# A state-space scan's softplus: the logarithm of 1 + u as a degree-nine polynomial, in the place of a reciprocal and an odd series

## The chip, the cores and the metric

The kernel runs on one core of one Trainium2 chip. The metric is device time in microseconds (us), of one execution of the whole program. It is the median of several runs.

A core has five engines that are used here, each with a queue of its own that it works through in order: TensorE (PE; its weight loads are shown as PEld), VectorE (DVE), ScalarE (ACT), GpSimd (POOL), and SyncE (SP), which only issues transfers here. They wait for one another by semaphores.

## What is computed

A decoder of four layers with twelve stages runs over x of 8 x 256 x 128 (float32). Each stage adds its result to x and normalises. The change is in the seventh stage, a selective state-space scan:

```python
def _L2_attn_ref(x, W_in, b_in, W_dt1, b_dt1, W_dt2, b_dt2, A, D):
    BC = x @ W_in + b_in                                  # N = 16 states
    Bm, Cm = (BC[..., :N], BC[..., N:])
    dt = jax.nn.softplus((x @ W_dt1 + b_dt1) @ W_dt2 + b_dt2)
    dt = jnp.clip(dt, 1e-07, 1000000.0)
    tmp = A * dt[..., None]
    A_bar = jnp.exp(tmp)
    B_barX = jnp.expm1(tmp) / tmp * dt[..., None] * Bm[:, :, None, :] * x[..., None]
    # h[s] = A_bar[s] * h[s-1] + B_barX[s], an associative scan along the sequence
    return jnp.sum(h * Cm[:, :, None, :], axis=-1) + D * x
```

The softplus of z is max(z, 0) + log(1 + u) with u = exp(-|z|), a number between 0 and 1.

## The kernel before

Each engine's program is written out by hand: for each stage a function gives this engine's instructions in their order, and semaphores named after the stage tie the engines together. The feed-forward stage ahead of the scan is `L1f`, the scan is `L2a`, and the next one is `L2x`.

**Tiling of the scan.** There are 8 batch rows b. For each, 128 channels lie on the partitions and 256 positions along the free dimension. The 16 states are taken in four chunks of four, so a chunk is a tile of 128 x 1024, and there are 32 chunks t = 4b + c. All engines' functions loop over `t in range(SCAN_FIRST, SCAN_LAST)`.

For each chunk, ACT scales x by B (`scaled`, L2288, eight instructions), PE transposes that into PSUM (`inputs`, L1729), and ACT makes the decay and half of the gain from the step size (`decays`, L2274 and L2275, eight instructions). DVE then forms the rest of the gain's factor (`feed`, L3091, reading `big` and PSUM), POOL multiplies (`gains`, L823 and L824), and DVE runs the scan (`scan`, L3099) and multiplies its result by C (L3103), which PE had spread over partitions in PSUM (`spread_c`, L1742). PE sums over the states (`summed`, L1758).

**Once per batch row**, ahead of need, the step size is made: PE projects (`scan_turn_x` L1645, `scan_project` L1650 and L1651, `scan_step_sizes` L1656 and L1658), ACT copies (L2227, L2237, L2238), and DVE adds the bias and so makes z (`scan_sized`, L2994 and L2997). ACT makes u (`scan_small_exponential`, L2245 and L2247), DVE makes the logarithm in two parts (`scan_ratio`, L3006 to L3009, and `scan_series`, L3014 to L3017), and then the softplus and its bounds (`scan_softplus`, L3031 to L3033). DVE also adds the residual and normalises (`residual` L3108, `deviations` L3114 and L3117, `norm` L3123).

`due(t, offset, 4)` gives the b for which t = 4b + offset. With the constants `SCAN_RATIO` = -6, `SCAN_SERIES` = -4 and `SCAN_DT` = -3, the ratio of row b stands behind the chunk 4b - 6, the series behind 4b - 4, and the softplus ahead of `feed` in the round 4b - 3. So DVE has two heavier rounds in each four: that with the ratio, and that with the series and the softplus. Row 0 is an exception: its whole logarithm and softplus stand at the end of `L1f`, and row 1's ratio ahead of the first `feed`.

`line.step(...)` is an instruction on DVE and a wait, also on DVE, for its end; `line.did(...)` is one without the wait. The ratio of the series is s = u / (u + 2), since log(1 + u) = 2 (s + s^3/3 + s^5/5 + ...); q is s squared, `s_of` is in the tile `resb`, `q_of` in `KT`, `series` in `xs`, and u in `OT`.

## Time and profile before

| | |
|---|---|
| median of 3 runs | 1869.52 us (1866.8 to 1877.95) |
| the profiled execution | 1869.56 us, of which the profile's span is 1867.8 us |
| PE busy | 1581.1 us, 85% of the span |
| DVE busy | 1295.2 us, 69% |
| ACT busy | 1055.6 us, 57% |
| POOL busy | 651.8 us, 35% |
| chain that ended last | PE 47%, DVE 23%, POOL 11%, issue 9%, ACT 8%, DMA 2% |

All times of an instruction are read from one profiled execution, counted from the start of its span. "Busy" is the time in which at least one instruction of an engine ran. Matmuls are pipelined and their ends are modelled, so that a busy PE is not one at its peak. PEclk is the clock that TensorE was granted, as a share of 2.4 GHz: 1.00 is that, and 0.50 is 1.2 GHz. The chain that ended last is followed back from the last instruction: at each step to what released it, or to the instruction before it on its engine. "[idle <- X]" behind an instruction is the time its engine had been idle before it, and the instruction that ended the idle time. The scan's part of the span lies between about 784 us, where the last rows of `L1f` overlap it, and 1040.5 us.

### The profile page before, as it was taken

To read this page: it belongs to the slowest core of one execution; us is meant where nothing else is said; L and a number is where in the kernel's file an instruction comes from. 1 tells how busy PE (TensorE), PEld (TensorE's weight loads), DVE (VectorE), ACT (ScalarE), POOL (GpSimd) and SP (SyncE) were. 2 spreads that over 40 slices of the span, in tenths; PEclk is the share of its full clock that TensorE was granted. 3 is DMA by queue.
4 is the path that set the end of the run, shared out by engine and by line. 5 is a ranking of instruction groups with operands and counts; after the bars stand their busy time and mean duration, and the time that the engine had idled before them with its cause. 6 is when DMAs were issued, how large, how long until landed. Compare 5 with 4: busy or idle time off the path is not lost.

```text
span 1867.8 us, 34707 instructions
## 1 busy us (share of the span) xinstructions
PE 1581.1 (85%) x12844; PEld 1135.7 (61%) x12847; DVE 1295.2 (69%) x2889; ACT 1055.6 (57%) x2177; POOL 651.8 (35%) x750
## 2 busy tenths in 40 slices
PE   6488857689998888889988899998899997978875
PEld 5244436568876555668777666665559974655542
DVE  2678862387776885679999467748844457468877
ACT  4388842267764775278787155537744442047645
POOL 3355525488884022445666213220000010001223
PEclk9699977899999999967888899999979998999985
DMA  3200121200000000000000100000000000000000
GB/s 118 109 13 12 35 86 34 57 10 1 1 1 1 2 2 1 4 34 1 1 1 1 55 2 2 2 12 1 2 1 1 1 10 1 1 18 2 2 1 23
DMA packets 14792, 30.95 MB, mean 17 GB/s; under 512 B 1537, under 2 KB 10145, under 8 KB 13857
## 3 DMA queue, kind: packets, MB, share of 16 engines
q1 hardware_dynamic: 13602, 26.63, 4.2%
q0 software_dynamic: 1024, 2.10, 0.4%
q8 instruction: 104, 1.70, 0.4%
q14 instruction: 62, 0.51, 0.1%
HBM read 22.42 MB, written 6.29 MB: 15 GB/s over the span
## 4 chain that ended last, share of the span: by engine, by line
PE 47%; DVE 23%; POOL 11%; issue 9%; ACT 8%; DMA 2%; SPq 0%; DVEq 0%; POOLq 0%; ACTq 0%
PE PS L1294 5%; PE PS L1354 4%; DVE negmax L2547 4%; POOL big L803 4%; DVE V L3099 3%; PE PS L1596 3%; PE PS L1607 3%; POOL big L791 3%; PE PS L1376 3%; ACT big L2066 2%; POOL big L799 2%; PE PS L1299 2%; ACT big L2044 2%; PE PS L1350 2%; PE PS L1368 2%
## 5 line engine op out<-in xcount | busy, mean ns | idle before, releaser
L2044 ACT ACTIVATE big<-PS 128x1024 f32<-128x1024 f32 (+1 forms) x256 | 248.2, 971 | 171.8 <-PE PS L1305 171.2
L2547 DVE TENSOR_REDUCE negmax<-PS 128x4 f32<-128x1024 f32 x192 | 234.9, 1224 | 59.3 <-PE PS L1294 58.2
L687 POOL TENSOR_TENSOR rstd<-veps,mhalf 128x2 f32<-128x2 f32 x72 | 51.7, 717 | 423.4 <-DVE veps L2430 423.0
L1294 PE MATMUL PS<-KS,QS 32*128 32x256 f32 (+1 forms) x1152 | 135.4, 320 | 50.3 <-DVE negmax L2547 37.1
L1294 PEld LDWEIGHTS PS<-KS,QS 32*128 32x128 f32 x1152 | 88.2, 189 | 127.3 <-DVE negmax L2547 88.7
L1354 PE MATMUL PS<-big,V 128*32 128x256 f32 (+1 forms) x2048 | 139.1, 392 | 0.7 <-ACT big L2044 0.4
L1305 PE MATMUL PS<-QS,KS 32*128 32x256 f32 (+1 forms) x1152 | 137.1, 326 | 0.6 <-ACT big L2044 0.6
L713 POOL TENSOR_TENSOR res<-resb,XB 128x256 f32<-128x256 f32 x24 | 17.4, 725 | 279.0 <-ACT resb L2130 279.0
L2566 DVE SCALAR_TENSOR_TENSOR QT<-PS,wint 128x1024 f32<-128x1024 f32 x64 | 77.2, 1219 | 30.1 <-PE PS L1247 30.0
L1305 PEld LDWEIGHTS PS<-QS,KS 32*128 32x128 f32 x1152 | 87.2, 192 | 6.0 <-issue 4.9
L755 POOL TENSOR_SCALAR KT<-QT 128x1024 f32<-128x1024 f32 x64 | 66.6, 1041 | 69.0 <-DVE QT L2566 67.1
L1758 PE MATMUL PS<-On,V 128*128 128x128 f32 x512 | 89.8, 348 | 0.8 <-DVE V L3103 0.8
L1758 PEld LDWEIGHTS PS<-On,V 128*128 128x128 f32 x512 | 83.3, 255 | 10.3 <-issue 9.3
L2209 ACT ACTIVATE QT<-PS,W 128x256 f32<-128x256 f32 x128 | 53.5, 470 | 59.4 <-PE PS L1596 59.4
L1376 PE MATMUL PS<-causal,identb 128*128 128x256 bf16 x595 | 85.9, 287 | 0.0
L1350 PE MATMUL PS<-big,V 128*32 128x512 f32 x512 | 67.7, 649 | 20.9 <-ACT big L2066 11.6
L1354 PEld LDWEIGHTS PS<-big,V 128*32 128x32 f32 x2048 | 55.4, 113 | 46.9 <-issue 18.7
L803 POOL TENSOR_TENSOR big<-big 128x512 f32<-128x512 f32 x64 | 81.2, 1269 | 5.0
L1023 PE MATMUL PS<-OT,W 128*128 128x256 f32 x272 | 73.3, 391 | 10.6 <-ACT QT L2001 10.6
L791 POOL TENSOR_SCALAR big<-big,rsum 128x256 f32<-128x256 f32 (+1 forms) x144 | 60.5, 432 | 62.4 <-DVE rsum L2477 62.3
L2288 ACT ACTIVATE QT<-x_tok,rt 128x128 f32<-128x128 f32 x256 | 77.8, 386 | 6.2 <-PE PS L1729 3.7
L1742 PE MATMUL PS<-OT,SEL 16*128 16x256 f32 x256 | 70.5, 418 | 11.6 <-DVE V L3103 11.6
(443 smaller groups left out, 4300.6 us busy)
## 6 DMA issues: line engine op xcount, KB each, us to landing
W<-in_wpack SPq DMA_DIRECT2D x1, 4180.0 KB, 12.3
W<-in_wpack SPq DMA_DIRECT2D x1, 2560.0 KB, 9.0
W<-in_wpack SPq DMA_DIRECT2D x1, 2449.5 KB, 9.6
y_rows<-one_more SPq DMA_DIRECT2D x1, 2048.0 KB, 10.6
masks<-in_mask SPq DMA_DIRECT2D x8, 256.0 KB, 2.8
x_rows<-x_tok SPq DMA_DIRECT2D x16, 128.0 KB, 2.0
W<-in_wpack SPq DMA_DIRECT2D x1, 1538.0 KB, 6.1
x_tok<-in_x SPq DMA_DIRECT2D x1, 1024.0 KB, 5.2
```

The costliest lines, as they stand in the source:

```text
L791: ins = nc.gpsimd.tensor_scalar(PRW[:, u % 4, c0:c1], PRW[:, u % 4, c0:c1], rsum[:, u % 16, j:j + 1], 1.0, ALU.mult, ALU.mult)
L803: nc.gpsimd.tensor_tensor(q, q, RTW[:, u % 4, :, :], ALU.add).then_inc(sem("t_rope"), 1)
L1294: mm = nc.tensor.matmul(PS[:, MAXB[half], o], QS[r, bm % 2, tm, j * P:(j + 1) * P], KS[r, bm % 2, tm, k], start=not a.causal, stop=last)
L1305: mm = nc.tensor.matmul(PS[:, exp_banks(ge)[half], o], KS[r, be % 2, te, kb * P:(kb + 1) * P], QS[r, be % 2, te, q], start=not a.causal, s ...
L1350: mm = nc.tensor.matmul(out_rows.rearrange("p (k c) -> p k c", k=2), v, PX_BOTH[:, :, T % 2, h, kb * S:(kb + 1) * S], start=first, stop=last)
L1354: mm = nc.tensor.matmul(out_rows[:, skip:S], v, PX[:, T % 2, h, kb * S:(kb + 1) * S - skip], start=first, stop=last)
L1376: nc.tensor.matmul(PS[:, bank, 0:S], identb[:, :], causal[:, 0, :], start=True, stop=True)
L1758: mm = nc.tensor.matmul(PS[:, YB, j * P:(j + 1) * P], chunk("h", t)[:, at:at + P], by_state[:, 4 * c + k, :], start=False, stop=c == 3 and ...
L2044: nc.scalar.activation(PX[:, T % 2, 2 * p:2 * p + 2, 0:cols], PS[:, exp_banks(g)[0]:exp_banks(g)[0] + 2, 0:cols], ACT.Exp, scale=a.scale). ...
L2288: ins = nc.scalar.activation(chunk("x", t)[:, at:at + P], x_tok[:, 2 * b + j, :], ACT.Copy, scale=B_cols(b)[:, i:i + 1])
L2547: ins = nc.vector.tensor_reduce(negmax[:, h:h + 2, :].rearrange("p h j -> p (h j)"), banks.rearrange("p h (j k) -> p (h j) k", j=2), AX.X, ...
L2566: nc.vector.scalar_tensor_tensor(clipped(QT, g), PS[:, pair_banks(g):pair_banks(g) + 2, :], -100.0 / a.scale, capT[:, g // PAIRS % 2, :].u ...
```

## The change

The logarithm is now a polynomial of degree nine in u itself, without a constant term. Two instructions give u * (c9 * u) and + c8 * u, and eight more each add a coefficient and multiply by u: ten instructions of the form SCALAR_TENSOR_TENSOR on 128 x 256, in place of four for the ratio (one of them a RECIPROCAL) and seven for the series. `scan_softplus` loses the instruction that formed 2s + s * series (L3031). The first five stand where the ratio was (`scan_logarithm_high`), and the other five where the series was (`scan_logarithm_low`). The separate increment of the semaphore `L2a_series` (L3017) is gone; the last of the ten increments it. u has two buffers in turn (the old tile in `OT`, and the place of q in `KT`), and ACT's wait before it writes u is for the polynomial of row b - 2 in place of the ratio of row b - 1. The intermediate tile `xT` and the places of s and q are no longer used here. Nothing else is changed on any engine.

```diff
@@ -220,6 +220,9 @@
 MASKED = -2.0 ** 100
 TURN_X_STEP, V_STEP, OT_STEP, Y_STEP = 6, 7, 2, 3
 STAGES = ORDER
+
+LOG1P = (0.999999994656, -0.499998926481, 0.333297104989, -0.249516162628, 0.196632742569,
+         -0.152696670739, 0.10543623795, -0.0563736128301, 0.0195425272629, -0.0031760570192)
 TURNED = [s for s in ORDER if s in ATTNS and ATTNS[s].turned_scores]
 
 
@@ -507,8 +510,11 @@
         def z_of(b):
             return OT[:, 6 + b % 2, :]
 
-        low_rank, u_of = OT[0:64, 4, :], OT[:, 5, :]
-        s_of, q_of, series = resb[:, :, :].rearrange("p j c -> p (j c)"), KT[:, 6, :], xs[:, :, :].rearrange("p j c -> p (j c)")
+        low_rank, series = OT[0:64, 4, :], xs[:, :, :].rearrange("p j c -> p (j c)")
+
+        def u_of(b):
+            return (OT[:, 5, :], KT[:, 6, :])[b % 2]
+
         diag, most = KT[:, 7, 0:P], KT[:, 7, P:P + 1]
         by_state = On[:, :, :].rearrange("p j (n c) -> p (j n) c", n=8)
 
@@ -2240,11 +2246,11 @@
 
             def scan_small_exponential(b):
                 act.wait_ge(sem("L2a_zdt"), b + 1)
-                if b:
-                    act.wait_ge(sem("L2a_q"), b)
-                nc.scalar.activation(u_of, z_of(b), ACT.Abs).then_inc(sem("L2a_absz"), 1)
+                if b >= 2:
+                    act.wait_ge(sem("L2a_series"), b - 1)
+                nc.scalar.activation(u_of(b), z_of(b), ACT.Abs).then_inc(sem("L2a_absz"), 1)
                 act.wait_ge(sem("L2a_absz"), b + 1)
-                nc.scalar.activation(u_of, u_of, ACT.Exp, scale=-1.0).then_inc(sem("L2a_u"), 1)
+                nc.scalar.activation(u_of(b), u_of(b), ACT.Exp, scale=-1.0).then_inc(sem("L2a_u"), 1)
 
             def L1f():
                 n = "L1f"
@@ -2996,25 +3002,22 @@
                                         w("L2a_brow").unsqueeze(1).broadcast_to([P, 2, 16]), ALU.add)
                 nc.vector.tensor_scalar(z_of(b), PS[:, 7, 0:S], w("L2a_bdt2"), None, ALU.add).then_inc(sem("L2a_zdt"), 1)
 
-            def scan_ratio(b):
+            def scan_logarithm_high(b):
 
 
                 dve.wait_ge(sem("L2a_u"), b + 1)
-                if b:
-                    dve.wait_ge(sem("L2a_series"), b)
-                s1 = xT[:, :]
-                line.step(nc.vector.scalar_tensor_tensor(s1, u_of, 2.0, u_of, ALU.add, ALU.max))
-                line.step(nc.vector.reciprocal(s1, s1))
-                line.step(nc.vector.tensor_tensor(s_of, u_of, s1, ALU.mult))
-                nc.vector.tensor_tensor(q_of, s_of, s_of, ALU.mult).then_inc(sem("L2a_q"), 1)
-
-            def scan_series(b):
-
-                dve.wait_ge(sem("L2a_q"), b + 1)
-                line.step(nc.vector.tensor_scalar(series, q_of, 2.0 / 15, None, ALU.mult))
-                for k in (13, 11, 9, 7, 5, 3):
-                    line.step(nc.vector.scalar_tensor_tensor(series, series, 2.0 / k, q_of, ALU.add, ALU.mult))
-                dve.sem_inc(sem("L2a_series"), 1)
+                u = u_of(b)
+                line.step(nc.vector.scalar_tensor_tensor(series, u, LOG1P[9], u, ALU.mult, ALU.mult))
+                line.step(nc.vector.scalar_tensor_tensor(series, u, LOG1P[8], series, ALU.mult, ALU.add))
+                for k in (7, 6, 5):
+                    line.step(nc.vector.scalar_tensor_tensor(series, series, LOG1P[k], u, ALU.add, ALU.mult))
+
+            def scan_logarithm_low(b):
+
+                u = u_of(b)
+                for k in (4, 3, 2, 1):
+                    line.step(nc.vector.scalar_tensor_tensor(series, series, LOG1P[k], u, ALU.add, ALU.mult))
+                nc.vector.scalar_tensor_tensor(series, series, LOG1P[0], u, ALU.add, ALU.mult).then_inc(sem("L2a_series"), 1)
 
             def scan_constants():
                 dve.wait_ge(*loaded("L2a"))
@@ -3028,8 +3031,7 @@
                 dve.wait_ge(sem("L2a_series"), b + 1)
                 if b >= 2:
                     dve.wait_ge(sem("L2a_decay"), 4 * (b - 1))
-                line.step(nc.vector.scalar_tensor_tensor(s_of, series, 2.0, s_of, ALU.add, ALU.mult))
-                line.step(nc.vector.scalar_tensor_tensor(z_of(b), z_of(b), 0.0, s_of, ALU.max, ALU.add))
+                line.step(nc.vector.scalar_tensor_tensor(z_of(b), z_of(b), 0.0, series, ALU.max, ALU.add))
                 nc.vector.scalar_tensor_tensor(step_size(b), z_of(b), 1e-7, most.broadcast_to([P, S]), ALU.max, ALU.min)\
                   .then_inc(sem("L2a_dt"), 1)
 
@@ -3074,8 +3076,8 @@
                         scan_constants()
                     elif b == 5:
                         scan_sized(0)
-                scan_ratio(0)
-                scan_series(0)
+                scan_logarithm_high(0)
+                scan_logarithm_low(0)
                 scan_softplus(0)
                 residual(B - 1)
 
@@ -3140,9 +3142,9 @@
                     if (b := due(t, SCAN_STEP_SIZE, 4)) is not None:
                         scan_sized(b)
                     if b := due(t, SCAN_RATIO, 4):
-                        scan_ratio(b)
+                        scan_logarithm_high(b)
                     if b := due(t, SCAN_SERIES, 4):
-                        scan_series(b)
+                        scan_logarithm_low(b)
                     if (b := due(t, SCAN_Y, 4)) is not None:
                         deviations(b)
 
```

In the listings below each row is an instruction of DVE's program: its line, its operation, the tile it writes <- those that it reads, its size, and how many like it follow one another. `xs` is the tile of the series or polynomial, `OT` and `KT` hold u, z and the step size, `resb` s, `V` the scan's result, `PS` is PSUM, `big`, `wint` and `one_more` hold decays, gains and their factors. Lines of the changed kernel are shifted: L3091 is now L3093, L3099 is L3101, L3103 is L3105, L3123 is L3125, L3108 is L3110.

DVE at the end of `L1f`, where row 0's logarithm and softplus are made, before:

```order
L3006 SCALAR_TENSOR_TENSOR xT<-OT 128x256
L3007 RECIPROCAL xT<-xT 128x256
L3008 TENSOR_TENSOR resb<-OT,xT 128x256
L3009 TENSOR_TENSOR KT<-resb 128x256
L3014 TENSOR_SCALAR xs<-KT 128x256
L3016 SCALAR_TENSOR_TENSOR xs<-xs,KT 128x256 x6
L3031 SCALAR_TENSOR_TENSOR resb<-xs,resb 128x256
L3032 SCALAR_TENSOR_TENSOR OT<-OT,resb 128x256
L3033 SCALAR_TENSOR_TENSOR KT<-OT,KT 128x256
```

The same place after the change:

```order
L3010 SCALAR_TENSOR_TENSOR xs<-OT 128x256
L3011 SCALAR_TENSOR_TENSOR xs<-OT,xs 128x256
L3013 SCALAR_TENSOR_TENSOR xs<-xs,OT 128x256 x3
L3019 SCALAR_TENSOR_TENSOR xs<-xs,OT 128x256 x4
L3020 SCALAR_TENSOR_TENSOR xs<-xs,OT 128x256
L3034 SCALAR_TENSOR_TENSOR OT<-OT,xs 128x256
L3035 SCALAR_TENSOR_TENSOR KT<-OT,KT 128x256
```

Fourteen instructions became twelve, and the reciprocal is gone; nothing moved past anything else.

DVE inside the scan, in the round of four that has the ratio (from the end of one chunk to the next `feed`), before:

```order
L3099 SCALAR_TENSOR_TENSOR V<-big 128x1024
L3103 TENSOR_TENSOR V<-V,PS 128x1024
L3006 SCALAR_TENSOR_TENSOR xT<-OT 128x256
L3007 RECIPROCAL xT<-xT 128x256
L3008 TENSOR_TENSOR resb<-OT,xT 128x256
L3009 TENSOR_TENSOR KT<-resb 128x256
L3123 SCALAR_TENSOR_TENSOR x_tok<-res,mv,rstd 128x128 x2
L3091 SCALAR_TENSOR_TENSOR one_more<-big,PS 128x1024
```

And after the change:

```order
L3101 SCALAR_TENSOR_TENSOR V<-big 128x1024
L3105 TENSOR_TENSOR V<-V,PS 128x1024
L3010 SCALAR_TENSOR_TENSOR xs<-KT 128x256
L3011 SCALAR_TENSOR_TENSOR xs<-KT,xs 128x256
L3013 SCALAR_TENSOR_TENSOR xs<-xs,KT 128x256 x3
L3125 SCALAR_TENSOR_TENSOR x_tok<-res,mv,rstd 128x128 x2
L3093 SCALAR_TENSOR_TENSOR one_more<-big,PS 128x1024
```

Four instructions became five, at the same place in the queue.

DVE in the round of four that has the series and the softplus, before:

```order
L3103 TENSOR_TENSOR V<-V,PS 128x1024
L3014 TENSOR_SCALAR xs<-KT 128x256
L3016 SCALAR_TENSOR_TENSOR xs<-xs,KT 128x256 x6
L3108 TENSOR_TENSOR res<-PS,x_tok 128x256
L3031 SCALAR_TENSOR_TENSOR resb<-xs,resb 128x256
L3032 SCALAR_TENSOR_TENSOR OT<-OT,resb 128x256
L3033 SCALAR_TENSOR_TENSOR KT<-OT,KT 128x256
```

And after the change:

```order
L3105 TENSOR_TENSOR V<-V,PS 128x1024
L3019 SCALAR_TENSOR_TENSOR xs<-xs,OT 128x256 x4
L3020 SCALAR_TENSOR_TENSOR xs<-xs,OT 128x256
L3110 TENSOR_TENSOR res<-PS,x_tok 128x256
L3034 SCALAR_TENSOR_TENSOR OT<-OT,xs 128x256
L3035 SCALAR_TENSOR_TENSOR KT<-OT,KT 128x256
```

Ten instructions and a separate increment became seven.

## Rows read from the trace of the kernel before

**Rows 1.** Busy time in a stretch: start:end, length, engines, PEclk, DMA, GB/s; the scan.
```profile
790.00:1040.50 250.50, 220.70 (x1134) 183.37 (x1134) 229.03 (x288) 188.11 (x538) 141.56 (x81) 0.79 0.02 7
```

**Rows 2.** The same view (PE, PEld, DVE, ACT, POOL): two rounds of four, then others.
```profile
883.65:913.27 29.62, 27.99 (x141) 23.61 (x140) 28.86 (x36) 22.47 (x66) 17.97 (x10) 0.77 0.00 1
913.27:942.89 29.62, 27.72 (x148) 23.49 (x147) 28.86 (x36) 25.70 (x75) 17.97 (x10) 0.80 0.00 1
1001.65:1023.23 21.58, 18.55 (x119) 16.32 (x120) 20.56 (x21) 18.06 (x50) 17.98 (x10) 0.92 0.00 1
808.00:828.00 20.00, 20.00 (x72) 15.94 (x71) 14.55 (x19) 17.32 (x51) 9.75 (x5) 0.51 0.01 1
```

**Rows 3.** Groups of DVE instructions by form, 853 to 972: busy, mean ns | idle.
```profile
L3103 DVE TENSOR_TENSOR V<-V,PS 128x1024 f32<-128x1024 f32 x16 | 19.5, 1221 | 0.6
```

**Rows 4.** Waits from 853 to 972: total us, times, longest.
```profile
ACT OT L2245 <- DVE OT L2997: 12.6, 4, 4.0
PE PS L1742 <- DVE V L3103: 4.5, 6, 1.6
```

**Rows 5.** Timeline of DVE, start and duration: the round with series and softplus.
```profile
877.93 1.15 DVE L3014 TENSOR_SCALAR xs<-KT 128x256 f32<-128x256 f32 x1
879.12 2.72 DVE L3016 SCALAR_TENSOR_TENSOR xs<-xs,KT 128x256 f32<-128x256 f32 x6
882.05 0.42 DVE L3108 TENSOR_TENSOR res<-PS,x_tok 128x256 f32<-128x256 f32 x1 [0.21 <-DVE xs L3016]
882.39 0.41 DVE L3031 SCALAR_TENSOR_TENSOR resb<-xs,resb 128x256 f32<-128x256 f32 x1
...
882.84 0.43 DVE L3032 SCALAR_TENSOR_TENSOR OT<-OT,resb 128x256 f32<-128x256 f32 x1
...
883.64 1.22 DVE L3091 SCALAR_TENSOR_TENSOR one_more<-big,PS 128x1024 f32<-128x1024 f32 x1
```

**Rows 6.** The chain that ended last, in order of time: two steps of the series.
```profile
880.03 0.44 DVE xs L3016
880.49 0.44 DVE xs L3016
```

**Rows 7.** Timeline of DVE and POOL: the round with the ratio.
```profile
890.01 2.28 DVE L3099 TENSOR_TENSOR_SCAN V<-big 128x1024 f32<-128x1024 f32 x1
...
890.28 4.18 POOL L824 TENSOR_TENSOR big<-big,wint 128x1024 f32<-128x1024 f32 x1
...
893.47 1.28 DVE L3006 SCALAR_TENSOR_TENSOR xT<-OT 128x256 f32<-128x256 f32 x1
...
894.78 1.75 DVE L3007 RECIPROCAL xT<-xT 128x256 f32<-128x256 f32 x1
...
897.37 0.61 DVE L3123 SCALAR_TENSOR_TENSOR x_tok<-res,mv,rstd 128x128 f32<-128x128 f32 x2
```

**Rows 8.** Timeline at the end of the stage before: row 0's logarithm and softplus.
```profile
785.43 0.42 DVE L3006 SCALAR_TENSOR_TENSOR xT<-OT 128x256 f32<-128x256 f32 x1
...
792.70 0.42 DVE L3033 SCALAR_TENSOR_TENSOR KT<-OT,KT 128x256 f32<-128x256 f32 x1
...
793.16 0.51 ACT L2274 ACTIVATE big<-KT,W 128x256 f32<-128x256 f32 x1 [3.37 <-DVE KT L3033]
```

**Rows 9.** Chain that ended last: one chunk's transposes, spreading and summing at PEclk 0.50.
```profile
813.18 3.71 PE PS L1742 x8
816.89 1.90 PE PS L1729 x8
...
824.07 3.41 PE PS L1758 x16
```

**Rows 10.** Timeline of DVE: where it waits for PE in the first chunks.
```profile
811.43 0.19 DVE L2994 TENSOR_TENSOR rt<-PS,W 128x32 f32<-128x32 f32 x1 [3.98 <-PE PS L1658]
...
832.23 1.22 DVE L3103 TENSOR_TENSOR V<-V,PS 128x1024 f32<-128x1024 f32 x1 [1.01 <-PE PS L1742]
...
843.99 4.00 DVE L3099 TENSOR_TENSOR_SCAN V<-big 128x1024 f32<-128x1024 f32 x1 [0.62 <-PE PS L1758]
```

## The prediction

> **What bounds the kernel now.** I first looked at where the changed instructions run. All of them are in the scan or in the last 5 us ahead of it, and the scan is 250.5 us of a span of 1867.8 us [rows 1]. Whatever the rest of the kernel is bound by, the change acts through the scan's length alone.
>
> Within the scan the busy times are PE 220.70, DVE 229.03, ACT 188.11 and POOL 141.56 us [rows 1]. DVE leads only a little, so the average decides nothing. I read it in pieces of one batch row (four chunks). From about 854 us on, such a piece takes 29.6 us, and DVE is busy for 28.86 us of it [rows 2]. The groups of DVE's instructions from 853 to 972 us show next to no idle time: 0.6 us over sixteen of L3103 [rows 3]. The waits point the same way: ACT waits 3.1 us per batch row for DVE's z (12.6 us in 4), and PE waits for DVE's scan result [rows 4]. So DVE sets this part's pace, up to about 1001 us. PE is a close second: 27.7 to 28.0 us busy in the same pieces, at a granted clock of 0.77 to 0.80.
>
> The first chunks are different. From 808 to 828 us PE is busy for all of 20.00 us at a granted clock of 0.51, DVE for 14.55 us [rows 2], and DVE waits for PE there: 3.98, 1.01 and 0.62 us [rows 10]. Before that, at 793 us, ACT stands still for 3.37 us until DVE's row-0 softplus is there [rows 8].
>
> **The change on DVE, per batch row.** The series ran from the start of L3014 at 877.93 to the residual at 882.05: 4.12 us [rows 5]. In this are six steps, and 0.21 us idle around the separate increment. A step that waits for the one before it takes 0.46 us from start to start (880.03 to 880.49) [rows 6]; an instruction of this size that nothing waits for gives way after 0.34 us (882.05 to 882.39) [rows 5]. The ratio ran from 893.47 to 897.37: 3.90 us [rows 7]. The softplus ran from 882.39 to 883.64: 1.25 us [rows 5].
>
> The first instruction of both parts is not at its own cost. L3006 took 1.28 us there [rows 7] and 0.42 us in row 0 [rows 8]. POOL's multiplication began at 890.28, behind the scan that had begun at 890.01, and ended at 894.46 [rows 7]. L3006 began at 893.47 and came to its end just behind that. I take it that an instruction with two SBUF inputs must wait for POOL's. The new first instructions also have two SBUF inputs, so they inherit this cost: 1.31 us to the next start (893.47 to 894.78). The Trainium skill ("SBUF — State Buffer", "SBUF: two separate sides") says that VectorE and GpSimd take a shared pair of ports exclusively, for the whole of an instruction, and that both an instruction in a two-port mode and one with two SBUF inputs are held. The trace agrees for L3006, and L3014 with its 1.15 us is the first kind.
>
> New cost of the first half: 1.31 + 4 x 0.46 = 3.15 us, saving 0.75. Of the second half: 1.31 + 3 x 0.46 + 0.34 = 3.03 us, saving 1.09. Of the softplus: 0.46 + 0.34 = 0.80 us, saving 0.45. Together 2.29 us of 29.62 in a batch row.
>
> All new instructions have a shape and form that the trace shows (L3016, L3006), so 0.42 us is a measured cost. The Trainium skill ("Vector Engine (DVE) Microarchitecture Reference", "Points that are easy to get wrong") says that this form with two SBUF sources that aren't bfloat16 runs at half throughput. This would speak against the change, which has two more of them per row (twelve for ten): at an estimated 0.27 us each (256 columns at 0.96 GHz, by the skill's "VectorE: DVE Perf Modes"), the saving would be 1.75 us instead of 2.29. But TENSOR_TENSOR L3108 and L3016 take the same 0.42 to 0.45 us here, so the row decides.
>
> **Where it counts.**
> - Row 0, at the end of the stage before: L3006 starts at 785.43 and L3033 at 792.70, 7.27 us [rows 8]. New: eleven steps of 0.46, or 5.06 us. ACT stands waiting for exactly this, so 2.21 us are on the path.
> - Row 1's first half (0.75) lies ahead of the first feed, and DVE then waits 3.98 us for PE [rows 10]. Row 1's second half (1.54 with the softplus) and row 2's first half (0.75) end in chunks in which DVE waits for PE at 832 and 844 us. I count these 3.04 us as nothing. They are covered by PE's work at the low clock.
> - Rows 2 to 7, second half and softplus: 6 x 1.54 = 9.24 us. Rows 3 to 7, first half: 5 x 0.75 = 3.75 us. All lie between 849 and 1001 us, where DVE sets the pace.
>
> Together 15.2 us.
>
> **ACT's changed wait and second buffer** cost nothing. ACT waited there for z anyway (3.1 us per row) [rows 4], and the new wait is for a polynomial that ended a whole batch row earlier. The old one was not late either.
>
> **What takes some of it back.** With 27.3 us per batch row, the others have less room. ACT needs at most 25.70 us [rows 2]. PE needs 27.7 to 28.0 at a clock of 0.77 to 0.80: more than the new period, if the clock stays. But at 0.92 it did four chunks in 21.58 us, with 18.55 busy [rows 2]; they lack only the projections of the next batch row. So PE at the high level has room, and at the low level it hasn't: one chunk then takes 3.71 + 1.90 + 3.41 = 9.02 us [rows 9] against 6.84 of DVE's. I expect DVE to wait now and then behind a stretch at 1.2 GHz. Such a wait can cost more than itself. At 843.99 the scan began 0.62 us late, came behind POOL's multiplication and took 4.00 us instead of 2.28 [rows 10, 7], 1.72 us more. The bounds are nothing (the clock rises with the denser work), and 8 us (such a wait of 0.62 + 1.72 us in three or four of the six batch rows). I take one, 2 us in round numbers, since the other clusters of low clock between 854 and 972 us made DVE wait for only 0.6 us in sixteen chunks.
>
> The Trainium skill ("TensorE: Matmul & The Clock Gate", "Part 1: The HAM clock gate") says that sustained activity releases the clock's throttle. By it the denser work would bring the high level, and the 2 us would fall away. The trace bears that out only in part: 0.92 in the dense piece from 1001.65, but 0.51 from 808 to 828 us, with PE busy all the time.
>
> Sum: 15.2 - 2 = 13.2 us. The profiled execution took 1869.56 us, practically the median (1869.52), so 1856.4, rounded to 1856 us, or 0.7% less.
>
> **Rivals.**
> - A, a chance of 14%: PE or ACT takes over. DVE's gain is mostly turned into waiting, because PE is at 28 of 29.6 us. What stays is row 0's 2.2 us and up to 5 more: 1862 to 1868 us. For it speaks the low clock of 0.77. Against it, PE itself waits for DVE, 4.5 us at L1742 in four batch rows, and keeps up.
> - B, 9%: the whole gain and the covered 3.0 us as well, 18.2 us, and the 2.2 us that row 0 gives let one more piece of the PE-bound start run at the high level. Going from 9.02 to about half of that in a chunk saves up to 4 us. This gives 1848 to 1851 us.
> - C, slower, 4%: the low clock, which held from 808 to 828 us, goes on further, since other work now falls at other times. Each chunk at the low level costs 9.02 us against the new 6.84, so 2.18 us of the gain. It decides from seven chunks more than now: 7 x 2.18 = 15.3 us. With ten more it would be 1876 us, and from sixteen on over 1% slower. Against it, the stretches at the low level were short once DVE set the pace.
> - That the change doesn't do what it says is hardly possible: fourteen dependent instructions become twelve on the engine that is busy for 28.86 of 29.62 us.
>
> **How the numbers follow.** The forecast, a gain of 8 to 18 us, has 73%. With A's and B's nearer parts, the range 1850 to 1866 us leaves out less than 2 in 10. About 1% (18.7 us) is what a measurement of this kernel can tell from no change. Beyond it on the fast side is almost only B, 9%. On the slow side is only C's far end, 2%. Within 1% is 89%.
>
> **What would show it.** In the new trace: ten instructions of 0.42 us, of which the first of each half takes 1.28 us inside the scan; the series' and residual's distance 3.0 us instead of 4.1; a batch row in 27.3 us, from `feed` to the fourth `feed` after it; ACT's wait for row 0's softplus about 1.2 us instead of 3.4; and the scan's last chunk about 13 us earlier. I'm wrong if the batch rows stay near 29 us with new DVE waits for L1742, L1758 or ACT's L2275, if scans of 4 us come up often, if a new instruction takes much more than 0.42 us, or if the granted clock of the scan changes from 0.79 by much.

## The result, and the profile after

| | before | after |
|---|---|---|
| median | 1873.74 us (4 runs, 1866.8 to 1884.34) | 1850.34 us (4 runs, 1842.41 to 1861.94) |
| ratio | | 0.9877, 95% interval 0.9834 to 0.9921 |
| profiled execution | 1869.56 us | 1852.06 us, span 1850.2 us |
| PE / DVE / ACT / POOL busy | 1581.1 / 1295.2 / 1055.6 / 651.8 us | 1560.4 / 1279.8 / 1056.8 / 653.3 us |

The changed kernel is 1.2% faster, some 23 us; a fourth run of the kernel before brought its median from 1869.52 to 1873.74 us. The prediction said 1856 us, 0.7% less than 1869.52, and a gain of 8 to 18 us. The measured 1850.34 us lies 0.34 us inside the lower end of its range (1850 to 1866), and the gain lies outside the 8 to 18 us.

The instructions cost what was predicted. This is the timeline of DVE (start, duration, instruction) after the change, first the round of four with the first half of the polynomial, then the one with the second half and the softplus:

```profile
895.00 1.28 DVE L3010 SCALAR_TENSOR_TENSOR xs<-OT 128x256 f32<-128x256 f32 x1
896.31 0.43 DVE L3011 SCALAR_TENSOR_TENSOR xs<-OT,xs 128x256 f32<-128x256 f32 x1
896.77 1.34 DVE L3013 SCALAR_TENSOR_TENSOR xs<-xs,OT 128x256 f32<-128x256 f32 x3
898.14 0.61 DVE L3125 SCALAR_TENSOR_TENSOR x_tok<-res,mv,rstd 128x128 f32<-128x128 f32 x2
...
908.34 2.67 DVE L3019 SCALAR_TENSOR_TENSOR xs<-xs,OT 128x256 f32<-128x256 f32 x4
911.04 0.43 DVE L3020 SCALAR_TENSOR_TENSOR xs<-xs,OT 128x256 f32<-128x256 f32 x1
911.38 0.42 DVE L3110 TENSOR_TENSOR res<-PS,x_tok 128x256 f32<-128x256 f32 x1
911.72 0.42 DVE L3034 SCALAR_TENSOR_TENSOR OT<-OT,xs 128x256 f32<-128x256 f32 x1
912.17 0.42 DVE L3035 SCALAR_TENSOR_TENSOR KT<-OT,KT 128x256 f32<-128x256 f32 x1
912.51 1.21 DVE L3093 SCALAR_TENSOR_TENSOR one_more<-big,PS 128x1024 f32<-128x1024 f32 x1
```

From 895.00 to 898.14 are 3.14 us (3.90 before, [rows 7]), from 908.34 to 911.38 are 3.04 us (4.12, [rows 5]), and from 911.72 to 912.51 are 0.79 us (1.25, [rows 5]). Together 6.97 us instead of 9.27.

Row 0 at the end of the stage before, on ACT and DVE, to be read against [rows 8]:

```profile
794.70 0.42 DVE L3010 SCALAR_TENSOR_TENSOR xs<-OT 128x256 f32<-128x256 f32 x1
795.15 0.56 DVE L3011 SCALAR_TENSOR_TENSOR xs<-OT,xs 128x256 f32<-128x256 f32 x1
...
800.01 0.42 DVE L3035 SCALAR_TENSOR_TENSOR KT<-OT,KT 128x256 f32<-128x256 f32 x1
...
800.47 0.51 ACT L2280 ACTIVATE big<-KT,W 128x256 f32<-128x256 f32 x1 [1.41 <-DVE KT L3035]
```

ACT's wait is down from 3.37 to 1.41 us. From the first instruction to the start of the last are 5.31 us instead of 7.27.

**Where the time went.** I divided both profiled executions at the same five events: the first instruction of row 0's logarithm, the first scan instruction (L3099 before, L3101 after; `TENSOR_TENSOR_SCAN` in the profile, though the listings ahead print it as `SCALAR_TENSOR_TENSOR`), the fifth, the twenty-ninth and the last. These are stretches of before (start:end, length, PE, PEld, DVE, ACT and POOL busy with counts, PEclk, DMA share, GB/s), and one batch row:

```profile
785.43:814.44 29.01, 15.92 (x61) 10.70 (x62) 17.97 (x47) 17.43 (x51) 6.48 (x7) 0.66 0.15 55
814.44:843.99 29.55, 29.55 (x120) 24.05 (x120) 26.57 (x29) 24.63 (x73) 17.77 (x10) 0.62 0.00 1
843.99:1018.50 174.51, 158.13 (x852) 133.34 (x851) 170.03 (x202) 146.91 (x422) 105.43 (x59) 0.83 0.00 1
1018.50:1034.35 15.85, 14.96 (x86) 12.90 (x86) 14.86 (x16) 1.59 (x4) 13.66 (x8) 0.89 0.01 2
874.47:904.10 29.63, 26.68 (x150) 22.53 (x151) 28.86 (x36) 24.04 (x70) 17.97 (x10) 0.88 0.00 1
```

And the same of after:

```profile
794.70:821.50 26.80, 15.67 (x60) 10.80 (x61) 15.38 (x47) 17.43 (x51) 6.76 (x7) 0.68 0.16 59
821.50:850.21 28.71, 28.71 (x131) 23.25 (x131) 25.93 (x28) 24.05 (x70) 15.33 (x8) 0.70 0.01 1
850.21:1010.88 160.67, 139.81 (x842) 115.31 (x841) 156.82 (x191) 146.51 (x421) 107.89 (x60) 0.93 0.00 1
1010.88:1026.52 15.64, 14.97 (x86) 12.90 (x86) 14.88 (x16) 2.55 (x7) 13.67 (x8) 0.89 0.01 1
877.56:904.89 27.33, 25.32 (x149) 20.75 (x148) 26.67 (x35) 24.16 (x70) 17.97 (x10) 0.90 0.00 1
```

The four differences are 2.21, 0.84, 13.84 and 0.21 us, or 17.1 us in all. A batch row takes 27.33 us, as worked out, and DVE is busy for 26.67 of it. DVE still sets the pace: from 853 to 990 us it waited 1.0 us for PE's L1748, while PE waited 15.0 us for DVE at the same line (waits of after: total us, times, longest):

```profile
PE PS L1748 <- DVE V L3105: 15.0, 9, 2.4
```

So it was PE's waiting that grew, and not DVE's: in the window of [rows 4], from 853 to 972 us, PE's wait for DVE at this line went from 4.5 to 12.6 us. The granted clock rose too: 0.93 instead of 0.83 in the long stretch. The clock doesn't set the length of these rows: before and pad have rows of 29.6 us at clocks from 0.69 to 0.88, the four profiles of after rows of 27.3 us at clocks from 0.88 to 0.97.

What the scan doesn't explain is that the first log instruction comes 9.3 us later in this execution of after, and that 9.8 us less lie behind the last scan. The code in both places is the same. The experiments had to tell whether this is chance.

### The profile page after: what moved, and what is told of

Read it like the earlier page. It is cut to its first block, busy times and chain, and to the rows that moved or that the text cites. A ratio compares the mean times of both kernels' runs of the same rounds, so it can differ in the third digit from the quotient of the medians.

```text
span 1850.2 us, 34682 instructions
## 1 busy us (share of the span) xinstructions
PE 1560.4 (84%) x12844; PEld 1115.3 (60%) x12847; DVE 1279.8 (69%) x2873; ACT 1056.8 (57%) x2177; POOL 653.3 (35%) x750
## 4 chain that ended last, share of the span: by engine, by line
PE 47%; DVE 22%; POOL 11%; issue 9%; ACT 9%; DMA 2%; SPq 0%; DVEq 0%; POOLq 0%; ACTq 0%
PE PS L1300 5%; PE PS L1360 4%; DVE negmax L2553 4%; POOL big L809 3%; PE PS L1602 3%; PE PS L1613 3%; DVE V L3101 3%; POOL big L797 3%; PE PS L1382 3%; PE PS L1356 2%; ACT big L2050 2%; POOL big L805 2%; ACT big L2072 2%; PE PS L1374 2%; PE PS L1305 2%
## 5 line engine op out<-in xcount | busy, mean ns | idle before, releaser
L1356 PE MATMUL PS<-big,V 128*32 128x512 f32 x512 | 72.7, 692 | 20.7 <-ACT big L2072 11.1
L1748 PE MATMUL PS<-OT,SEL 16*128 16x256 f32 x256 | 72.6, 428 | 17.2 <-DVE V L3105 17.2
L2294 ACT ACTIVATE QT<-x_tok,rt 128x128 f32<-128x128 f32 x256 | 77.8, 386 | 3.4 <-PE PS L1699 2.5
L2072 ACT ACTIVATE big<-KT,W 128x1024 f32<-128x1024 f32 x64 | 73.2, 1144 | 8.6 <-POOL KT L761 8.6
L2007 ACT COPY QT<-PS 64x256 f32<-64x256 f32 x128 | 47.0, 367 | 52.8 <-DVE big L2467 51.1
```

Of the source, the lines that this page charges most:

```text
L1356: mm = nc.tensor.matmul(out_rows.rearrange("p (k c) -> p k c", k=2), v, PX_BOTH[:, :, T % 2, h, kb * S:(kb + 1) * S], start=first, stop=last)
L2072: nc.scalar.activation((PX, PX2)[k][:, T % 2, 2 * p:2 * p + 2, :], clipped((QT, KT)[k], g), ACT.Exp, scale=a.scale, bias=w(("high_base", " ...
L2294: ins = nc.scalar.activation(chunk("x", t)[:, at:at + P], x_tok[:, 2 * b + j, :], ACT.Copy, scale=B_cols(b)[:, i:i + 1])
```

## The experiments

All ran with the kernel before beside them on the same chip. "Ratio" is that to before, with its 95% interval.

### Both kernels again: same_before and same_after

No edit. These give the spread of executions, and more profiles.

> The kernel before, unchanged, as a measure of what differs from execution to execution. Every theory: a ratio to the kernel before of 1.00. Open, and the reason for the run: how far the scan's length (from the first L3006 to the end of the last L3103: 252.5 us in the profiled execution of before, 235.4 us from the first L3010 to the end of the last L3105 in that of after) and the rest of the program (9.3 us longer ahead of the scan and 9.8 us shorter behind it in the profiled execution of after) vary where nothing is changed. Theory 1 (what lies outside the scan is chance, the change is worth the scan's 17 us): the parts ahead of and behind the scan differ by up to 10 us between two executions of the same kernel too. Rival (the change also shortens what follows the scan): the part behind the scan stays at about 829.9 us here, within 3 us.

> The changed kernel, unchanged, a second time. Theory 1 (DVE's time in the scan and row 0's 2.2 us, plus the start of the scan that came through with more TensorE clock): 17 us less than before, ratio 0.991; from the first L3010 to the end of the last L3105 235 to 238 us; granted clock of the scan 0.85 to 0.90 against 0.79. Rival (over 1% is gained, by something behind the scan too): ratio 0.988 or lower again, and the part behind the scan is near 820 us again.

same_before: ratio 0.9995 (0.9964 to 1.0026), 12 runs from 1852.92 to 1873.98 us. same_after: 0.9883 (0.9849 to 0.9916), 1838.21 us median against 1861.56. The first scan and the last stand here (duration min/median/max in ns, first and last start), for same_before and then for same_after:

```profile
L3099 DVE TENSOR_TENSOR_SCAN V<-big x32: 2278/2284/2285, 807.3 to 1024.8; 128x1024 f32<-128x1024 f32 x32
```

```profile
L3101 DVE TENSOR_TENSOR_SCAN V<-big x32: 2277/2284/4258, 807.8 to 1012.7; 128x1024 f32<-128x1024 f32 x32
```

This is 217.5 us against 204.9; from the first log instruction to the first scan it is 29.0 (778.3 to 807.3) against 26.6 us (781.2 to 807.8). What the scan and row 0 explain is then 15.0 us here, and 17.1 us in the first pair. The parts outside vary: in same_before the part ahead of the scan is 7 us shorter than in before. So theory 1 holds for that part: over all thirteen profiles of this document the first log instruction comes anywhere from 778.2 to 794.7 us, though the program ahead of it is the same in each. The part behind the last scan was 835.6 us in same_before, 2 us from before, and 820.7 us in same_after. Both numbers that the rival named came (a ratio near 0.988, and near 820 us behind the scan), so it stands, and after_third, before_fourth and after_fourth come back to it.

### The saved time put back: pad

```diff
+                for k in range(2):
+                    line.step(nc.vector.scalar_tensor_tensor(xT[:, :], series, 1.0, u, ALU.add, ALU.mult))
...
+                for k in range(3):
+                    line.step(nc.vector.scalar_tensor_tensor(xT[:, :], series, 1.0, u, ALU.add, ALU.mult))
```

> After, with five more steps of the same form (128x256, two SBUF inputs, result in a tile that nobody reads) in each batch row: two in the first half, three in the second, 5 x 0.46 = 2.30 us, as much as the change saved there. Theory 1 (the gain is DVE's time in the scan): back to before, ratio 0.998 to 1.002, a batch row of 29.6 us, first L3010 to the last L3105's end about 252 us. Rival 1 (the reciprocal itself, or its neighbours, disturbed other engines, or the second buffer of u did it): some of the gain stays, ratio 0.99. Rival 2 (the granted clock follows how dense PE's work is): clock of the scan back at 0.79, which theory 1 alone doesn't ask for.

Measured: 0.9991 (0.9963 to 1.0019). A batch row takes before's 29.6 us again. Stretches of pad, the first four chunks and one batch row (the one with the lowest clock; the others had 0.77 to 0.88):

```profile
811.72:840.53 28.81, 28.81 (x131) 23.35 (x131) 26.09 (x33) 24.04 (x70) 17.21 (x8) 0.70 0.00 1
899.78:929.41 29.63, 28.39 (x133) 24.37 (x132) 28.79 (x40) 24.09 (x70) 18.00 (x10) 0.69 0.00 1
```

With twice the buffers for u, without a reciprocal, and with the time put back, nothing of the gain is left that can be measured. It is DVE's time that counts. Rival 1 falls. Rival 2 holds as an addition, since the clock goes down again when the time is put back: over the whole scan it was 0.80 in pad, 0.80 to 0.83 in three profiles of before, and 0.86 to 0.89 in four of after.

### Still less on DVE: short

```diff
-                for k in (7, 6, 5):
-                    line.step(nc.vector.scalar_tensor_tensor(series, series, LOG1P[k], u, ALU.add, ALU.mult))
...
-                for k in (4, 3, 2, 1):
+                for k in (1,):
```

The kernel leaves out six of the polynomial's ten steps.

> After, with three of the ten polynomial steps left out of each half (the logarithm is wrong, which is what is left out): 6 x 0.46 = 2.76 us less on DVE per batch row. Theory 1 (DVE still sets the pace after the change): 5 x 1.38 + 6 x 1.38 + row 0's 2.76 = 18 us less than after, ratio to before about 0.979, a batch row of 24.6 us. Rival (PE or ACT has taken over, since ACT needs 24.6 us and PE 23.4 us at the full clock): at most half of it, 9 us, ratio 0.984 to 0.990, with DVE's waits for L1748 or L2281 in the trace.

Measured: 0.9807 (0.9774 to 0.984), 14.1 us less than same_after in the medians. Two batch rows of short:

```profile
856.88:881.73 24.85, 24.47 (x142) 20.72 (x141) 24.35 (x28) 23.94 (x70) 17.99 (x10) 0.86 0.01 2
881.73:906.31 24.58, 24.21 (x148) 20.17 (x147) 24.27 (x28) 23.67 (x69) 18.00 (x10) 0.93 0.00 1
```

The steady batch rows are 24.6 to 24.9 us, as theory 1 asked, with DVE busy for 24.3 of it. The 32 scans lie within 190.5 us instead of 204.9, 14.4 us less; 15.2 were expected. Of row 0's 2.76 us less than half came through (25.5 us to the first scan against 26.6): ACT no longer waits for the softplus there, and begins with the decays 1.7 us after DVE has begun the last instruction of it, because it is still busy with L2294. So DVE still leads at 27.3 us, and only near 24.6 us are PE (24.2 to 24.5 us busy) and ACT (23.7 to 23.9) level with it.

### Row 0 alone: row0

```diff
-                scan_ratio(0)
-                scan_series(0)
-                scan_softplus(0)
+                dve.wait_ge(sem("L2a_u"), 1)
+                line.step(nc.vector.scalar_tensor_tensor(series, u_of, LOG1P[9], u_of, ALU.mult, ALU.mult))
...
```

The rest of the ten steps and the softplus' two follow inline; rows 1 to 7 are made as before.

> The kernel before, with the polynomial for row 0 alone, at the end of the stage before (rows 1 to 7 keep the reciprocal and the series). Theory 1 (row 0's chain is on the path, since ACT stands waiting for it): from the first logarithm instruction to the first scan 2.2 us less than in before (there 29.0 us: 785.43 to 814.44), so 26.8 us, and from the first scan to the last one as before, 217 to 220 us. Rival (something else sets the first feed): 29 us remain.

Measured, in a single execution: the first log instruction starts at 779.0 us and the first scan at 805.6, so 26.6 us. From there to the last scan are 218.5 us, as in before. Row 0's two microseconds are on the path, and they don't need the rest of the change. Its 1860.4 us against 1865.68 is within what single executions differ.

### POOL's multiplication taken away: nopool

```diff
-                    nc.gpsimd.tensor_tensor(chunk("gain", t), chunk("gain", t), fed_to(t), ALU.mult).then_inc(sem(f"{n}_gain"), 1)
+                    nc.gpsimd.tensor_tensor(chunk("gain", t)[:, 0:4], chunk("gain", t)[:, 0:4], fed_to(t)[:, 0:4], ALU.mult).then_inc(sem(f"{n}_gain"), 1)
```

The kernel leaves out the multiplication of all but four columns of each chunk's gain.

> After, with POOL's multiplication of the gain cut from 1024 columns to 4 (the rest of the gain is what is left out). Theory 1 (the first instruction of each half takes 1.28 us instead of 0.42 only because it waits for POOL's multiplication): L3010 and the first L3019 of each row take 0.42 to 0.43 us in the scan too, and a batch row takes 27.33 - 2 x 0.86 = 25.6 us, unless ACT's 24.6 us or PE intervene; ratio to before about 0.982. Rival (they are slow for another reason, such as the PSUM instruction right ahead of them): 1.28 us and 27.3 us remain.

Measured: 0.9847 (0.9797 to 0.9898). DVE's timeline in nopool, at the second half and then at the first half of a polynomial:

```profile
895.43 1.22 DVE L3105 TENSOR_TENSOR V<-V,PS 128x1024 f32<-128x1024 f32 x1 [1.25 <-PE PS L1748]
896.57 1.80 DVE L3019 SCALAR_TENSOR_TENSOR xs<-xs,OT 128x256 f32<-128x256 f32 x4
...
909.70 0.42 DVE L3010 SCALAR_TENSOR_TENSOR xs<-KT 128x256 f32<-128x256 f32 x1
910.15 0.42 DVE L3011 SCALAR_TENSOR_TENSOR xs<-KT,xs 128x256 f32<-128x256 f32 x1
```

L3010 takes 0.42 us instead of 1.28, and the four of L3019 1.80 us instead of 2.67. So the 0.86 us belong to POOL's multiplication and not to the PSUM instruction ahead, which is still there. Batch rows came down to 25.6 us, as worked out, but two of the five to 26.8 and 26.5 us:

```profile
866.28:891.90 25.62, 25.34 (x140) 21.22 (x140) 25.10 (x34) 24.05 (x70) 9.44 (x10) 0.83 0.00 1
891.90:918.72 26.82, 24.94 (x154) 20.33 (x154) 25.09 (x34) 24.16 (x70) 9.43 (x10) 0.95 0.00 1
```

The second of these holds the wait of 1.25 us for PE that stands above. At this length rival A of the prediction begins: PE, busy for 25.3 of 25.6 us, is at times late.

### The halves put where POOL is done: moved and moved2

```diff
-SCAN_X, SCAN_PROJECT, SCAN_STEP_SIZE, SCAN_U, SCAN_RATIO, SCAN_SERIES, SCAN_DT, SCAN_Y, SCAN_DONE = -11, -10, -9, -8, -6, -4, -3, 5, 7
+SCAN_X, SCAN_PROJECT, SCAN_STEP_SIZE, SCAN_U, SCAN_RATIO, SCAN_SERIES, SCAN_DT, SCAN_Y, SCAN_DONE = -11, -10, -9, -8, -7, -5, -3, 5, 7
...
-                    if b := due(t, SCAN_RATIO, 4):
-                        scan_logarithm_high(b)
                     if b := due(t, SCAN_SERIES, 4):
                         scan_logarithm_low(b)
                     if (b := due(t, SCAN_Y, 4)) is not None:
                         deviations(b)
+                    if b := due(t, SCAN_RATIO, 4):
+                        scan_logarithm_high(b)
+                    if (b := due(t, SCAN_Y, 4)) is not None and b <= B - 4:
+                        norm(b)
```

> After, in another order on DVE: the first half of the polynomial one round earlier, behind the residual's statistics (0.7 us of work with one SBUF input, under which POOL's multiplication ends), the second half one round earlier, behind the making of z (0.45 us that read PSUM), and the normalisation behind the first half. Same instructions. Theory 1 (POOL's multiplication costs 0.86 us at each half because of where the halves stand): of 1.72 us per batch row some 1.2 to 1.3 go, a batch row of 26.1 us, 7 us less than after in all, ratio to before about 0.984. Rival 1 (PE or ACT limits rounds that are now only 4.6 us long): at most 3 us less than after. Rival 2: DVE's instructions now meet POOL elsewhere, and nothing is gained.

Measured: 0.9856 (0.9818 to 0.9893), beside 0.9879 (0.9831 to 0.9927) for after on the same chip. The first instruction of the first half came down to 0.59 us, where statistics stand ahead of it. In moved, DVE's timeline and then two batch rows:

```profile
926.36 0.48 DVE L3116 BATCH_NORM_STATS2 stats<-res 128x6 f32<-128x128 f32 x2
926.88 0.25 DVE L3119 BATCH_NORM_AGGREGATE mv<-stats 128x2 f32<-128x6 f32 x2
927.04 0.59 DVE L3010 SCALAR_TENSOR_TENSOR xs<-OT 128x256 f32<-128x256 f32 x1
```

```profile
889.41:916.67 27.26, 26.46 (x156) 21.66 (x155) 25.77 (x34) 24.42 (x72) 18.35 (x10) 0.92 0.00 1
943.57:970.28 26.71, 24.23 (x133) 20.42 (x132) 25.75 (x32) 25.73 (x75) 18.34 (x10) 0.81 0.00 1
```

DVE's busy time fell to 25.75 us per batch row, by 0.9 us and not by the 1.2 to 1.3 us of theory 1, and the rows took 26.7 to 27.3 us. Two groups of DVE's instructions in moved, from 840 to 990 us (busy, mean ns | idle before, and what ended it), say where the rest went:

```profile
L3034 DVE SCALAR_TENSOR_TENSOR OT<-OT,xs 128x256 f32<-128x256 f32 x6 | 5.1, 854 | 0.0
L3105 DVE TENSOR_TENSOR V<-V,PS 128x1024 f32<-128x1024 f32 x23 | 28.1, 1221 | 2.7 <-PE PS L1748 2.0
```

The softplus' first instruction, L3034, takes 0.85 us where it took 0.42 us in after: with the second half gone from ahead of it, it is now the one that waits for POOL. In five of the six rounds it ends 0.3 us behind POOL's multiplication (rival 2, in part). And ahead of L3105, the instruction with PE's spread C, DVE stood idle for 2.7 us, 2.0 of them waiting for L1748, in rounds that are only 4.6 us long; another 0.7 us went ahead of the residual, for L1764. That is rival 1, and by these waits it took some 0.6 of the 0.9 us that a batch row had gained. The first chunks became longer too: 35.1 us from the end of the last transposes of `L1f` (L1699) to the first scan, where after takes 33.6, and 29.49 us to the fifth. In the latter is a wait of DVE for ACT:

```profile
826.94 1.22 DVE L3093 SCALAR_TENSOR_TENSOR one_more<-big,PS 128x1024 f32<-128x1024 f32 x1 [3.17 <-ACT big L2281]
```

In moved2, rows 2 to 7 keep moved's order, and row 1's two halves go back to where after has them.

> The order of moved for rows 2 to 7, and that of after for row 1, whose two halves in moved held up the first feeds (35.1 us to the first scan and 29.5 us to the fifth, against 33.6 and 28.6 in after). Theory 1 (row 1's halves belong under PE's work at the low clock): 33.6 and 28.6 us again, later batch rows of 26.8 to 27.0 us as in moved, 2.3 us less than moved and 5 to 6 us less than after; ratio to before about 0.984. Rival (the first chunks wait for PE whatever DVE does): as moved, 0.986.

Measured: 0.9856 (0.9811 to 0.9901). The way to the first scan was 33.7 us again, but the next four chunks took 30.70 us, longer than in moved (29.49) or after (28.5 to 28.7). My reason for row 1 was right for the way to the first scan and wrong for the chunks after it, where DVE waited 2.12 us for ACT's L2281 again. What made moved2 longer than moved is a third place, in the last four chunks, where moved has no such wait:

```profile
1005.70 0.42 DVE L3110 TENSOR_TENSOR res<-PS,x_tok 128x256 f32<-128x256 f32 x1 [1.90 <-PE PS L1764]
```

By their scans with the way to them, moved and moved2 gain 2.6 and 0.8 us on after; in the timings neither is told apart from after, though both are faster than before.

### Both kernels again: after_third, before_fourth and after_fourth

> The changed kernel once more, unchanged, for the size of the gain and for one more profile. The scan explains 15.4 to 17.3 us so far, and the two measurements gave 22 to 23 us (ratios 0.9877 and 0.9883). Theory 1 (all of the gain is made up to the end of the scan, the rest is chance in where PE's low clock falls): ratio 0.990 to 0.992, and the stretch from the last scan to matmul 6200, at the start of the next stage, is sometimes longer than 33.2 us. Rival (some 5 us more come from there, systematically: 33.2 and 33.2 us in the two profiles of after, 39.3 and 36.7 in the two of before): ratio 0.988 again and 33.2 us again.

> The kernel before, unchanged, for one more profile. Theory 1 (what lies behind the scan depends on how the program stands to the clock's changes, not on the kernel): from the last scan to matmul 6200 any of 33.2 to 39.3 us; ratio 1.00. Rival (before always loses time there): over 36 us again.

> The changed kernel, unchanged, for one more profile and for the size of the gain on the same chip as before_fourth and moved2. Theory 1: in the scan 204.9 us from the first to the last scan instruction and 33.6 us ahead of it, as three times before; from the last scan to matmul 6200 between 33.2 and 39.3 us; ratio 0.988 to 0.992. Rival: 33.2 us again.

after_third: 0.9879 (0.9831 to 0.9927). before_fourth: 0.9998 (0.9963 to 1.0032). after_fourth: 0.9893 (0.9846 to 0.994). With the first result and same_after, after was measured four times: 0.9877, 0.9883, 0.9879, 0.9893. So the gain is 20 to 23 us. The profiles account for less up to the last scan: 17.1 us in the first pair, 15.0 in the second, 17.8 with before_fourth and after_fourth. Each interval alone would still allow that; the four together put the gain at some 19 to 25 us (an estimate from all their runs), which is more. after_third's ratio also lies outside the 0.990 to 0.992 of theory 1.

The scan of after was the same in all four profiles to 0.1 us (205.0, 204.9, 204.9, 205.0); before's was 219.9, 217.5 and 220.4, and row0's 218.5. For the part behind the last scan, whose code is the same everywhere, one stretch each of before_fourth, row0, pad and after_fourth. DVE, ACT and POOL are busy for the same time in all four, within 0.7 us; what differs is PE's busy time, and the clock:

```profile
1042.25:1868.50 826.25, 723.89 (x6848) 502.36 (x6846) 546.50 (x1301) 407.76 (x692) 124.86 (x160) 0.92 0.02 8
```

```profile
1024.15:1858.70 834.55, 730.51 (x6845) 505.88 (x6846) 546.46 (x1301) 407.06 (x692) 124.57 (x160) 0.92 0.02 8
```

```profile
1029.74:1850.80 821.06, 717.92 (x6845) 500.61 (x6846) 546.45 (x1301) 407.23 (x692) 124.56 (x160) 0.93 0.02 8
```

```profile
1025.15:1845.00 819.85, 715.92 (x6848) 498.61 (x6846) 546.29 (x1301) 407.11 (x692) 124.57 (x160) 0.94 0.02 8
```

| | last scan to end of span | last scan to matmul 6200 |
|---|---|---|
| before, same_before, before_fourth | 833.5, 835.6, 826.3 us | 39.3, 36.7, 34.6 us |
| row0, pad (scan as long as before's) | 834.6, 821.1 us | 33.2, 33.7 us |
| after, same_after, after_third, after_fourth | 823.7, 820.7, 823.6, 819.9 us | 33.2, 33.2, 33.1, 33.2 us |
| short, nopool, moved, moved2 (scan shorter than after's) | 826.0, 825.5, 820.3, 817.6 us | 34.6, 34.5, 34.5, 33.2 us |

Theory 1 as I wrote it falls in one point: after always had the short 33.2 us, at a granted clock of 1.00 throughout. The rival falls too, as "before always loses time there": it asked for over 36 us in before_fourth (34.6 came), and row0 and pad, with a scan as long as before's, had 33.2 and 33.7 us. What it said of after came each time. What is left is this. Outside the scan the length depends on where the clock is low; before and its like range from 821 to 836 us, after from 820 to 824, and the four kernels with a shorter scan still from 818 to 826. Whether after meets the good case more often for a reason, or in four draws by chance, stays open. It would account for the remaining 5 us or so.

## Why the prediction was right, and where it was off

- **What bounds the scan.** Right: DVE. pad gave the whole gain back, and short went on gaining at the full rate.
- **The cost of the new instructions.** Right to 0.01 us per half: 3.14, 3.04 and 0.79 us against 3.15, 3.03 and 0.80. The batch row of 27.33 us was right too. The half throughput for this form, which the Trainium skill ("Vector Engine (DVE) Microarchitecture Reference", "Points that are easy to get wrong") states, shows in none of these runs: where POOL held none of them up, the ten steps took 0.42 to 0.43 us each, as long as TENSOR_TENSOR of this size.
- **The first instruction's 0.86 us.** Right, and by nopool shown to be POOL's multiplication. It was an inference before.
- **Row 0.** Predicted 2.21 us, measured 2.2 in the first pair of profiles and 2.4 to 2.5 in the others (26.6 us in row0 against 29.0). But the chain itself gave only 1.96 us, from 7.27 to 5.31, the same within 0.01 us in every pair: two of the steps were held up beside POOL's normalisation (0.56 us for L3011 at 795.15), so that ACT's remaining wait was 1.41 us and not 1.2. The other 0.3 to 0.5 us came between the softplus and the first scan, where I had no term; that the first pair hit 2.21 is luck.
- **Rows 2 to 7.** Predicted 13.0 us, measured 13.0 us in the second pair (173.64 to 160.63). In the first it was 13.8 (174.51 to 160.67), since before had a scan of 4.00 us in this stretch.
- **What I counted as nothing.** The first four chunks gained 0.84 us in the first pair, 0.3 and 1.4 in the two others; the end of the scan gained 0.2 us in two pairs and lost 0.8 in the second.
- **The term that was wrong: "I take one, 2 us", for waits behind PE at the low clock.** It was nothing: the full batch rows took 27.3 us in all four profiles of after, and no scan from the fifth on was late. The step behind it took PE's 28 us busy in 29.6 us as work that stays. But that busy time holds the slow half of the clock. When DVE got faster, the same matmuls of the scan took 183.5 to 189.5 us busy instead of 197.6 to 203.1, and the granted clock went from 0.80 to 0.83 up to 0.86 to 0.89.
- **The clock.** The Trainium skill ("TensorE: Matmul & The Clock Gate", "Part 1: The HAM clock gate") says that sustained activity releases the throttle. By that rule the 2 us would have fallen away, as they did; but the first four chunks stayed at 0.70 with PE busy all of the 28.71 us.
- **The chances, and luck.** A gain of over 1% had 9%, and it came, at 1.2%. Within the scan and on the way to it the sum of 15.2 us held, with 15 to 18 us. The other 5 us or so lie outside, where I had no term and where no run shows a cause. I had set the range from a median of 1869.52 us, as if that were fixed; in the later measurements the kernel before, run beside it, had medians of 1861.56, 1865.68 and 1865.03 us and the changed one 1838.21, 1842.91 and 1846.86 us, all three below 1850. So the time fell into the range by luck. What was right is the mechanism, and the part of the gain that it makes. With executions of one kernel from 1852.7 to 1875.2 us, I gave the band inside 1% far too much.
- **Rivals.** A (PE takes over) did not come at 27.3 us; it begins near 25 us, as nopool and short show. B was the nearest in size, but not by its mechanism: of the covered 3.0 us only 0.3 to 1.4 us came, the first four chunks still ran at 0.70 to 0.71 (0.61 to 0.70 before), and the rest came from outside the scan. C did not come.

## What to carry to other kernels

When one engine sets the pace and another is close behind with a low granted clock, don't take the second one's busy time for a floor, since its clock may rise when it is fed faster. Don't take its best stretch for a floor either: four chunks took PE 18.55 us busy at 0.92 [rows 2], but whole batch rows at 0.83 to 0.95 kept it busy for 24.2 to 25.3 us in short and nopool. Count dependent steps by their distance from start to start, price separately the first instruction that stands behind a long one of POOL (1.28 us here instead of 0.42), and check both against rows of the same form. When you move such an instruction away, look at which one takes its place behind POOL. An instruction saved counts only where the engine has no cover: look for whom the others wait, in each part of the stage.

## What the runs showed of the hardware that I had not expected

- A VectorE step that waits for the one before it took 0.46 us from start to start on 128 x 256 [rows 6], and an instruction of this size that the next one doesn't wait for 0.34 us [rows 5]. Here a dependence cost 0.12 us.
- RECIPROCAL on 128 x 256 float32 took 1.75 us [rows 7], as much as four multiply-adds of the same size (0.42 us each). Ten fused operations beat a reciprocal and eleven others.
- A scan instruction whose POOL multiplication had started first took 3.9 to 4.3 us instead of 2.28. It came up once in seven of the thirteen profiles, each time behind a short wait of DVE for PE: in before and before_fourth at the fifth scan, in all four of after and in short at the third. In same_before, row0, pad, nopool, moved and moved2 it didn't.
- The scan's length in after was the same to 0.1 us in four profiles whose other parts differed by 13 us, while before's differed by 3 us.
